# A fused DeepFM and CIN kernel: a shorter setup, four look-ups a tile, a last tile of its own, three row buffers

## The reference

```python
emb = embed_table[f_ix, x_idx]                        # 2048 x 26 x 16
lin1 = w1_table[f_ix, x_idx].sum(axis=1, keepdims=True) + w1_bias
s = emb.sum(axis=1)
fm = 0.5 * ((s * s).sum(-1) - (emb * emb).sum(axis=(1, 2)))[:, None]
h = relu(emb.reshape(n, F * D) @ mlp_w1 + mlp_b1)     # 416 -> 400
h = relu(h @ mlp_w2 + mlp_b2)                         # 400 -> 400
deepfm = lin1 + fm + h @ mlp_w3 + mlp_b3
x0 = emb.transpose(0, 2, 1); last = x0
for W in (cin_w0, cin_w1, cin_w2):                    # 128 x {26 or 128} x 26
    last = einsum('ndl,ndf,klf->ndk', last, x0, W); feats.append(last)
y = deepfm + concatenate(feats, -1).sum(axis=1) @ lin_w + lin_b
```

## Time and profile before

| | |
|---|---|
| median of 3 runs | 530.3 us (530.12 to 530.62) |
| profiled execution | 530.45 us |
| its span in the trace | 528.6 us |
| busy: PE, DVE, ACT, POOL | 468.6, 376.7, 361.6, 364.6 us |
| instructions: PE, DVE, ACT, POOL | 2230, 610, 707, 382 |
| mean granted clock of TensorE | 0.968 |

### The profile page before, as it was taken

How to read it: one execution, slowest core, us unless ns; L and a number is a source line. 1 busy time by engine, 2 the same in 40 slices (tenths; PEclk the granted TensorE clock), 3 DMA queues, 4 the chain that set the end, 5 groups by cost and what they waited for, 6 DMA issues and landing times. The chain is left out here.

```text
span 528.6 us, 6627 instructions
## 1 busy us (share of the span) xinstructions
PE 468.6 (89%) x2230; PEld 384.6 (73%) x2230; DVE 376.7 (71%) x610; ACT 361.6 (68%) x707; POOL 364.6 (69%) x382
## 2 busy tenths in 40 slices
PE   0798499899898989899999989898989899998895
PEld 0795367588787878687877878787868687787684
DVE  6811265869687786868686968778686868695766
ACT  1002459878686877777676868786777767677883
POOL 5777787877777777777777777777777777774000
PEclk9999559899999999999999999999999999999998
DMA  8973652122222222222222222222222222221000
GB/s 179 237 133 26 82 132 8 5 8 7 9 7 9 7 8 7 9 7 9 7 8 7 8 8 8 8 8 8 8 8 8 8 8 7 8 8 6 0 2 1
DMA packets 21550, 13.63 MB, mean 26 GB/s; under 512 B 12792, under 2 KB 20493, under 8 KB 21261
## 3 DMA queue, kind: packets, MB, share of 16 engines
q0 software_dynamic: 12064, 3.31, 18.4%
q1 hardware_dynamic: 5863, 7.92, 6.4%
q10 hardware_dynamic: 3590, 1.99, 2.0%
HBM read 13.00 MB, written 0.19 MB: 25 GB/s over the span
## 5 line engine op out<-in xcount | busy, mean ns | idle before, releaser
L417 POOL DMA_INDIRECT emb<-rows,idx_raw x377 | 364.3, 966 | 117.4 <-issue 114.6
L660 DVE TENSOR_TENSOR z_lo<-ps_s,z_hi 128x512 fp32r<-128x512 f32 (+1 forms) x192 | 130.7, 687 | 66.5 <-ACT ps_s L483 65.1
L476 ACT ACTIVATE z_hi<-ps_s 128x512 fp32r<-128x512 f32 (+1 forms) x192 | 114.4, 596 | 78.7 <-PE ps_s L908 77.8
L483 ACT ACTIVATE ps_s<-ps_s 128x512 f32<-128x512 f32 (+1 forms) x192 | 113.9, 593 | 0.7
L922 PE MATMUL ps_q<-z_lo,zw_hi 128*127 128x512 f32 (+1 forms) x192 | 86.0, 448 | 15.9 <-DVE z_lo L660 14.4
L923 PE MATMUL ps_q<-z_hi,zw_lo 128*127 128x512 f32 (+1 forms) x192 | 76.4, 398 | 0.0
L924 PE MATMUL ps_q<-z_hi,zw_hi 128*127 128x512 f32 (+1 forms) x192 | 76.3, 397 | 0.0
L908 PE MATMUL ps_s<-xt,pick 128*128 128x512 f32 (+1 forms) x192 | 74.3, 402 | 0.4 <-DVE xt L652 0.4
L922 PEld LDWEIGHTS ps_q<-z_lo,zw_hi 128*127 128x127 f32 (+1 forms) x192 | 36.4, 190 | 32.4 <-DVE z_lo L660 19.7
L994 PE MATMUL ps_y<-look_hi,one_hot 128*128 128x442 f32 (+1 forms) x156 | 56.3, 361 | 2.3 <-DVE one_hot L754 2.3
L995 PE MATMUL ps_y<-look_lo,one_hot 128*128 128x442 f32 (+1 forms) x156 | 54.8, 353 | 0.0
(11 more groups left out here) (165 smaller groups left out, 757.2 us busy)
## 6 DMA issues: line engine op xcount, KB each, us to landing
emb<-rows,idx_raw POOLq DMA_INDIRECT x377, 3.0
w_space<-rows SPq DMA_DIRECT2D x2, 728.9 KB
m_raw<-mlp_w SPq DMA_DIRECT2D x2, 650.0 KB
w<-cin_w SPq DMA_DIRECT2D x1, 832.0 KB, 6.7
w<-cin_w ACTq DMA_DIRECT2D x1, 832.0 KB, 13.2
w_space<-cin_w SPq DMA_DIRECT2D x1, 832.0 KB, 15.0
w_space<-cin_w ACTq DMA_DIRECT2D x1, 832.0 KB, 18.4
m_raw<-rows SPq DMA_DIRECT2D x1, 728.9 KB
```

Source lines behind the costliest of these rows:

```text
L417: pool.indirect_dma_start(emb[t % EMB][:, f, :], None, rows, bass.IndirectOffsetOnAxis(row_ix[:, t, f:f + 1], 0)).then_inc(gathered[t], 16)
L476: act.activation(z_hi[0:k, c, :], ps[0:k, :], ACT.Square)
L483: act.activation(ps[0:k, :], ps[0:k, :], ACT.Square).then_inc(hi_ready, 1)
L660: dve.tensor_tensor(z_lo[0:k, u % NC, :], ps_s[s_no(t, u) % RING][0:k, :], z_hi[0:k, u % NC, :].bitcast(F32), ALU.subtract).then_inc(lo_re ...
```

## The change

Setup:
- `cin_w2` comes in two halves of its output columns, each with its own semaphore; PE multiplies 64 columns at a time (52 matmuls). SP no longer waits for the indices ahead of it, and `cin_w1` is issued only when the first half is there.
- `move` is one DMA for a whole block, six in all, out of scratch that `leave` (six stores in place of three) has laid out in that order.
- The keys of all tiles are transposed by one matmul, stored to DRAM, and read back by one DMA a tile, spread over the partitions. The matmul `keys` goes away, and `one_hot` is made from SBUF.
- The second layer's weights are loaded, split and stored later (in tile 0), in three full chunks of 128 rows and a rest of 16, for which low and high parts lie in one chunk (`m2_rest`): `hidden2` has 10 matmuls in place of 12. ACT and DVE get a second, small instruction each at `hidden1_high` and `hidden1_low`, and ACT one at `hidden1`.

Tiles:
- Four look-ups in place of three, in other steps. POOL issues 364 gathers, not 377. The fourth row is picked in `start_tile`, ahead of step 0's `z_lo`.
- Three row buffers in place of four; the linear terms are summed (`sum_first`) at the end of `start_tile`, not in step 9.
- `x_high` makes only `xt`; the full copy `x32` (`x_full`) stands behind the square of step 0, and PE's `picked` of steps 1 and 2 waits for it.
- The last tile: its rows are copied in three parts, behind tile 14's square of step 11, the last part when the last four gathers are in. PE transposes them after all of tile 14, and DVE does its share in the order of `start_last`.

Core of the diff:

```diff
-LOOKS = 3
+LOOKS = 4
+EARLY = 18
-        EMB = 4
+        EMB = 3
...
-        ROWS = {3: 0, 7: 1, 11: 2}
+        ROWS = {3: 0, 6: 1, 8: 2, 11: 3}
...
-            for a in range(GROUPS[g]):
-                eng.dma_start(moved[a * n_c:(a + 1) * n_c, g, col:col + n_b * n_d].rearrange("c (b d) -> c b d", d=n_d),
-                              bass.AP(src.tensor, src.offset + offset + a * st_a, [[st_c, n_c], [st_b, n_b], [1, n_d]])
-                              ).then_inc(moved_in[g], 16)
+            eng.wait_ge(y_stored[n], 16)
+            eng.dma_start(moved[0:n_a * n_c, g, col:col + n_b * n_d].rearrange("p (b d) -> p b d", d=n_d),
+                          bass.AP(y_dram[n].tensor, y_dram[n].offset,
+                                  [[n_d, n_a * n_c], [n_a * n_c * n_d, n_b], [1, n_d]])).then_inc(moved_in[g], 16)
...
-            sp.wait_ge(idx0_in, 16)
-            sp.dma_start(w2[0:HALF_P], cin_w2[0:HALF_P]).then_inc(w2_in, 16)
+            for h in range(2):
+                ls = slice(HALF_P * h, HALF_P * (h + 1))
+                sp.dma_start(w2[0:HALF_P, ls], cin_w2[0:HALF_P, ls]).then_inc(w2_in[h], 16)
+            sp.wait_ge(w2_in[0], 16 * 2)
...
             def start_tile(t):
                 x_high(t, 0)
                 x_high(t, 1)
-                for u in range(NC):
-                    square(t, u)
+                square(t, 0)
+                x_full(t, 0)
+                x_full(t, 1)
+                square(t, 1)
+                square(t, 2)
+                sum_first(t)
...
+            def start_last():
+                t = T - 1
+                times_left(t - 1, NQ - 1)
+                times_third(t - 1)
+                add_third(t - 1)
+                add_product(t - 1, NQ - 1)
+                fold(t - 1)
+                hidden2(t - 1)
+                x_low(t, 0)
+                x_low(t, 1)
+                for u in range(NC):
+                    z_low(t, u)
...
             def keys_to_one_hot(t, i):
-                dve.wait_ge(keys_out, look_no(t, i) + 1)
-                dve.tensor_tensor(one_hot[:], ps_y[:, 0:P].unsqueeze(1).to_broadcast([P, SHARES, P]),
+                if i == 0:
+                    dve.wait_ge(keys_in[t % 2], 16 * ((t - FIRST_LOOK) // 2 + 1))
+                if look_no(t, i):
+                    dve.wait_ge(rows_out, look_no(t, i))
+                dve.tensor_tensor(one_hot[:], key_row[t % 2][:, i:i + 1, :].to_broadcast([P, SHARES, P]),
...
+                if u in (1, 2):
+                    pe.wait_ge(x32_ready, 2 * t + u)
...
                 else:
+                    if after == T - 1:
+                        hidden2(t)
+                        sum_products(t)
+                        x_half(after, 0)
+                        x_half(after, 1)
                     picked(after, 0)
```

More of the change, by code:

```diff
@@ L129, in deepfm_cin_kernel @@
     XK = LO + XR
-    HC = H // 4
+    HR = H - 3 * P
+    REST = LO + HR + 1
     HALF_P = P // 2
@@ L206, in deepfm_cin_kernel @@
         look_place = sb("look_place", [P, T, LOOKS])
+        room_b = sb("room_b", [P, 2 * LOOKS * P])
+        key_row = [room_b[:, b * LOOKS * P:(b + 1) * LOOKS * P].rearrange("p (i n) -> p i n", i=LOOKS) for b in range(2)]
+        key_t = sb("key_t", [T * LOOKS, P])
         one_hot = sb("one_hot", [P, SHARES, P], F32R)
@@ L401, in _ @@
                     "(p c) r -> p (c r)", c=LAST)).then_inc(look_in[i], 16)
+            sp.wait_ge(keys_stored, 16)
+            for n in range(3, 6):
+                sp.wait_ge(y_stored[n], 16)
+            for t in range(FIRST_LOOK, T):
+                if t >= FIRST_LOOK + 2:
+                    sp.wait_ge(one_hot_ready, look_no(t - 2, LOOKS))
+                sp.dma_start(key_row[t % 2], key_dram[LOOKS * t:LOOKS * (t + 1), :].partition_broadcast(P)
+                             ).then_inc(keys_in[t % 2], 16)
             sp.wait_ge(y_ready, 1)
@@ L440, in _ @@
             act.wait_ge(idx0_in, 16)
-            act.dma_start(w2[HALF_P:P], cin_w2[HALF_P:P]).then_inc(w2_in, 16)
+            for h in range(2):
+                ls = slice(HALF_P * h, HALF_P * (h + 1))
+                act.dma_start(w2[HALF_P:P, ls], cin_w2[HALF_P:P, ls]).then_inc(w2_in[h], 16)
+            act.wait_ge(w2_in[0], 16 * 2)
             act.dma_start(w1[HALF_P:P], cin_w1[HALF_P:P]).then_inc(w1_in, 16)
@@ L725, in tile @@
                         look_low(LOOK_SPLIT[u - 2])
+                    if t == 0 and u == 10:
+                        second_low()
                     if looks(t + LEAD):
@@ L842, in _ @@
         def _(pe):
-            pe.wait_ge(w2_in, 16 * 2)
             pe.wait_ge(lin_in, 16 * 3)
-            for g in range(F):
-                mm = pe.matmul(ps_y[:, g:g + 1], w2[:, :, g], lin[:, 2:3], start=True, stop=True)
+            for h in range(2):
+                ls = slice(HALF_P * h, HALF_P * (h + 1))
+                pe.wait_ge(w2_in[h], 16 * 2)
+                for g in range(F):
+                    mm = pe.matmul(ps_y[ls, g:g + 1], w2[:, ls, g], lin[:, 2:3], start=True, stop=True)
             mm.then_inc(m_done, 1)
@@ L1049, in _ @@
                     if looks(t + LEAD):
-                        if u in KEYS:
-                            keys(t + LEAD, KEYS[u])
                         if u in ROWS:
                             look_rows(t + LEAD, ROWS[u])
-                    if after is not None:
+                    if after is not None and after < T - 1:
                         if u == 9:
```

265 lines of the change are left out of this document (165 added, 100 removed).

## The result

The changed kernel takes 558.82 us (median of 4 runs, 556.91 to 559.52), the kernel before 530.21 us in the same comparison: ratio 1.0533, interval 1.0506 to 1.0560. Forecast were 550.0 us and a range of 529 to 557. The direction is right and so is the mechanism of the tiles with look-ups; the size is 9 us short, the time lies outside the range, and in the setup, in tile 0 and at the last crossing a step of the forecast failed. The profiled execution took 559.52 us, its span is 557.6, so the terms are compared with the forecast span of 548.2.

A forecast was written before the change was run, and what follows sets the result against it. PE was taken as the bound, with waits where DVE or ACT is late. Span 528.6 - 11 (setup) + 3 (tile 0) + 23.4 (13 tiles) + 4.5 (last tile) - 0.3 (tail) = 548.2, forecast 550 us, range 529 to 557.

The forecast's parts named there:

- The tile with look-ups: Each of 13 tiles with look-ups takes 1.8 us more, +23.4 us in all; bounds 0 and 2.6 a tile.
- steps 1 to 5: PE's waits in a tile: 1.25 us at the second look-up, 0.45 third, 0.85 fourth, 0.6 + 0.3 for full copies.
- the walk: A tile's instructions timed from step 2's `main`: next step 2 at 30.5 us, 28.7 for the old order.
- The setup: Everything before tile 0, with halved `cin_w2` and single moves: -11 us, bounds 0 and -15.
- Product done at 22.5: Setup: PE's first product ends at 22.5, not 28.0, with `cin_w2` in halves: 5.5 us gained, bounds 0 and 7.
- Gain 4.5 + 0.9 = 5.4 us: Setup's DRAM trip with single moves: first group 4.5 us earlier, 0.9 wait between groups gone; bounds 0 and 8.
- Tile 0: First tile: ACT gets more copies and loses the linear sum, +3 us, bounds 2 and 6.
- what ACT gets there counts: Tile 0: ACT is busy 14.94 of 16 us, so its added copies (two of 1.6 us, two small) lengthen the tile.
- The last crossing: Tile 14 to tile 15: drained pipeline, step 2 about 13 us after the last `main`, not 8.5: +4.5, bounds 2 and 6.
- Absorbed waits: Rival: PE's new waits in tiles are absorbed, the tile stays at 28.6 us, 526.7 us in all; chance 0.15.
- POOL paces: Rival: PE's waits shrink but `one_hot` holds POOL's gathers, which set the tiles' pace: 523 to 540 us; chance 0.09.
- The single moves bring nothing: Rival, setup: many short pieces drain as slowly as 9 DMAs: +5, 555 us; no chance of its own given.

The follow-up runs named there:

- Experiments 1 and 2: Changed kernel with look-ups two and three behind steps 7 and 9: 538.16 us; with all four look-ups behind steps 2, 4, 7, 11: 530.74 us.
- experiment 6: Kernel before with both setup parts (halves of `cin_w2`, single moves) and nothing else: 521.14 us, 0.9825 of the kernel before.
- experiment 7: Changed kernel with the key store behind the moves and `t_moved` in SP's queue: whole time not measured (disturbed chip), DRAM trip 13.81 and 13.99 us.

## Why the prediction was right in kind and short in size

- **The tile with look-ups: right, and the calibration was the error.** Each wait of steps 1 to 5 is in the trace and ends within 0.15 us of where the walk has it; singly they differ by up to 0.2 us, and that the sum comes out at 30.55 against 30.5 is in part luck. I then charged only 30.5 - 28.7, since the same walk (not written out in the prediction) gave 28.7 for the old order where the trace has 28.57. Against the measured 28.57 the new walk says +1.93 a tile, +25.1 in all, and +25.8 were measured. Experiments 1 and 2 show that these waits, and no engine's load, are the loss.
- **The setup: -11 forecast, -7.8 measured.** "Product done at 22.5" was right (PE left L970 at 22.7). The failed step is the DRAM trip's "Gain 4.5 + 0.9 = 5.4 us", added to the 5.5 as if independent: in the changed kernel the trip and the wait between groups gave 2.4. Each part was nearly right alone (5.7 and 4.8); together they give 9.2 (experiment 6), and the key store, which the prediction named among the stores and gave no price, costs the trip 0.5 us or more (experiment 7). What the rest is stays open.
- **Tile 0: +3 forecast, +4.6 measured.** The failed step is "what ACT gets there counts". I added the fourth table to ACT and forgot the subtraction that goes with it on DVE, which stands ahead of the next tile's `x_low`; PE's idle time then was followed by a lower clock, which the sum did not hold. The bounds of 2 to 6 do hold it, by luck.
- **The last crossing: +4.5 forecast, +6.8 measured.** Step 2 came 16.2 us behind tile 14's last `main`, not 13. From 530.09 to 534.78 eleven matmuls at 0.43 instead of 0.23 us are 2.2 of these 3.2 us. The prediction counted that the pipeline is drained and not what the clock does when PE idles, though the earlier trace rows showed just that for the setup. The miss would be larger, had not tile 14 up to its last `main` become 1.1 us shorter (15.11 instead of 16.17 us).
- **Absorbed waits** (rival, 526.7): no. Nothing was given back but the 0.81 us at the old L941, which was in the walk.
- **POOL paces** (rival, 523 to 540): no, 0.5 us of holds a tile instead of up to 2.4. But POOL is near: in experiment 6, with three look-ups, its last gather starts at 481.85 and ACT takes those rows at 485.64, by the 3 us used before some 0.8 us after they land (an estimate). With tiles much shorter than that the fourth look-up might begin to be worth something; no run here shows it.
- **The single moves bring nothing** (rival, 555): no, 4.8 us alone.
- **The range** failed since its upper end stood only 7 us above the forecast, less than the setup's own bound of 0 would allow, while four terms missed by 1.6 to 3.2 us each and all in one direction. Two of them share a cause that the sum left out, the lower clock behind an idle PE.

## What to carry to other kernels

Walk a hand-written order in absolute time and trust the walk's own total: where it is 0.1 us off the trace for the old order, that is its error, and not a correction that the new order shares. The first look at a look-up, gather or copy that stands early or late should be at what its consumer's order asks: here three lines of numbers were worth 28 us of 559, with not one instruction more or less. And read from the trace which engine's queue ends a wait last: in tile 0 it was DVE's, where the forecast had loaded ACT's. Price any stretch in which PE idles twice, once for the idle time and once for the clock behind it, and don't add two gains of one chain of transfers without asking what each was hiding. Two kernels that reach a point at the same time need not lose the same things on the way there.

## What the runs showed of the hardware

- A pass of PE costs by the columns of its load: 104 passes with 64 columns took 11.54 us (0.111 each), 52 with 128 columns 11.91 (0.229 each). The Trainium skill (TensorE: Matmul & The Clock Gate, LDWEIGHTS (loading the stationary operand)) says that the load's time goes by its columns; the trace agrees for these two widths, and so splitting the output in halves cost PE nothing.
- TensorE's granted clock fell without one long stop of PE. In 518.60 to 528.90 PE had 4.81 us of work in 10.30, its longest stops were 2.20 and 2.25 us, and the clock went from 1.00 to 0.50, where it stayed for the 5.88 us behind; in tile 0 it was 0.96 in 95.00 to 98.40, which holds a stop of 2.24 us, and 0.51 in the 3.2 us behind.
- A gather was held by a DVE instruction with two SBUF operands only if it began inside it: 1.30 and 1.12 us instead of 0.94 beside a `one_hot` of 0.68 us, and none of those that had begun before. The `one_hot` took 0.67 to 0.68 us in either case.
- One DMA in place of nine is dearer to issue: three took 2.69 us on SP's queue and 1.84 on ACT's, 0.9 and 0.6 each, where one of the small ones takes 0.375; the six stores ahead of them (`leave`) take 0.72 each.
